# First mixture of experts of a two-layer decoder: order of the mask rows, wide maskings, and hidden values masked by TensorE

## The reference, cut to what matters

```
scores = sigmoid(x @ gate_w.T);  sel = top_2(scores + expert_bias)        # 8 experts
routed = x[token of each choice] * normalised_score
xq   = mxfp8_qdq(routed)                 # blocks of 32: power-of-two scale, float8 payload
h13  = ragged_dot(xq, w13q^T, counts);   h = silu(h1) * h3
hq   = mxfp8_qdq(h)
routed_out = ragged_dot(hq, w2q^T, counts)      # each row by the expert that it chose
shared = (silu(x @ sw1.T) * (x @ sw3.T)) @ sw2.T
out = shared + sum over the two choices of routed_out
```

## Time and profile before

| what | value |
|---|---|
| median of 3 runs | 1411.94 us (1411.03 to 1414.29) |
| profiled execution | 1419.62 us |
| its span | 1417.8 us |
| mean granted TensorE clock | 0.929 |
| busy share PE / DVE / ACT / POOL | 85% / 62% / 39% / 34% |

### The profile page before, as it was taken

How to read it: one execution, slowest core, us unless ns; L and a number is a source line. 1 busy time by engine, 2 the same in 40 slices (tenths; PEclk the granted TensorE clock), 3 DMA queues, 4 the chain that set the end, 5 groups by cost and what they waited for, 6 DMA issues and landing times.

```text
span 1417.8 us, 21841 instructions
## 1 busy us (share of the span) xinstructions
PE 1202.7 (85%) x7071; PEld 806.6 (57%) x7071; DVE 878.5 (62%) x2229; ACT 557.5 (39%) x1460; POOL 478.3 (34%) x584
## 2 busy tenths in 40 slices
PE   7688998999879959899999989998999409889881
PEld 3554664667744447466774356634667307777770
DVE  1677887753498993766637877587764523444443
ACT  2246776885351101377300167513772302212210
POOL 2253763743100002355400044301442362444444
PEclk9899999999969979899979999999999758999996
DMA  7065996000001001100030000003103523444544
GB/s 293 27 225 171 310 327 191 17 1 1 31 1 44 1 1 75 60 1 2 1 127 1 0 1 1 1 1 131 78 1 119 213 95 69 81 80 81 86 69 108
DMA packets 69612, 110.72 MB, mean 78 GB/s; under 512 B 5056, under 2 KB 59840, under 8 KB 66240
## 3 DMA queue, kind: packets, MB, share of 16 engines
q1 hardware_dynamic: 58896, 96.62, 20.2%
q0 software_dynamic: 10608, 12.72, 5.8%
HBM read 57.41 MB, written 51.91 MB: 77 GB/s over the span
## 4 chain that ended last, share of the span: by engine, by line
PE 66%; DVE 17%; issue 6%; POOL 4%; DMA 3%; ACT 2%; another core or an unknown queue 1%; SPq 1%; POOLq 0%; DVEq 0%; ACTq 0%
PE ps L701 8%; PE ps L690 6%; PE ps L979 6%; PE ps L710 4%; PE ps L682 4%; PE ps L683 3%; PE ps L1033 3%; PE ps L1030 3%; PE ps L960 2%; PE ps L650 2%; PE ps L812 2%; POOL mem L1839 2%; PE ps L864 2%; PE ps L884 2%; PE ps L1049 1%
## 5 line engine op out<-in xcount | busy, mean ns | idle before, releaser
L1839 POOL TENSOR_SCALAR mem<-mem 128x512 f32<-128x512 f32 x256 | 178.4, 701 | 383.9 <-DVE mem L1172 380.6
L1167 DVE TENSOR_REDUCE mem<-ps 128x1 f32<-128x512 f32 x256 | 175.2, 687 | 106.6 <-PE ps L683 98.1
L1665 ACT ACTIVATE mem<-ps,mem 128x512 f32<-128x512 f32 x256 | 177.3, 697 | 13.2 <-DVE mem L1167 12.6
L690 PE MATMUL ps<-mem 128*128 128x128 f32 x1024 | 158.0, 277 | 14.3 <-POOL mem L1839 13.4
L690 PEld LDWEIGHTS ps<-mem 128*128 128x128 f32 x1024 | 117.4, 140 | 69.2 <-POOL mem L1839 51.0
L1658 ACT ACTIVATE mem<-ps 128x512 f32<-128x512 f32 x192 | 116.2, 606 | 90.2 <-PE ps L690 89.7
L1890 POOL DMA_INDIRECT sums<-mem x63 | 97.1, 1542 | 133.1 <-DVE mem L1527 113.5
L682 PE MATMUL ps<-rounded_at 128*128 128x512 f32 x256 | 124.5, 486 | 10.9 <-DVE rounded_at L1156 10.4
L701 PE MATMUL ps<-mem 128*64 128x256 f32 x1024 | 124.6, 385 | 2.4 <-ACT mem L1658 2.4
L1633 ACT ACTIVATE rounded_at<-ps 64x512 fp32r<-64x512 f32 x64 | 37.9, 592 | 165.8 <-PE ps L962 153.0
L683 PE MATMUL ps<-rounded_at 128*128 128x512 f32 x256 | 102.3, 400 | 0.0
(11 more groups left out here) (259 smaller groups left out, 2464.0 us busy)
## 6 DMA issues: line engine op xcount, KB each, us to landing
slots<-mem SPq DMA_DIRECT2D x15, 2312.0 KB, 10.3
mem<-in_f_w_dram SPq DMA_DIRECT2D x16, 1024.0 KB, 9.0
mem<-slots SPq DMA_DIRECT2D x63, 136.0 KB
mem<-in_f_w_dram SPq DMA_DIRECT2D x24, 256.0 KB, 3.3
mem<-in_x_wq_dram SPq DMA_DIRECT2D x2, 2048.0 KB, 13.2
mem<-in_x_wo_dram SPq DMA_DIRECT2D x2, 2048.0 KB, 8.4
mem<-sums SPq DMA_DIRECT2D x8, 256.0 KB, 4.2
mem<-in_x_wqr_dram SPq DMA_DIRECT2D x1, 1536.0 KB, 6.7
```

The costliest lines, as they stand in the source:

```text
L690: mm = pe.transpose(ps[3 + j % 2][:, k * P:(k + 1) * P], PR[j % 6][:, k * P:(k + 1) * P], ident)
L1167: dve.tensor_reduce(nmax[:, i % 8:i % 8 + 1], ps[SB[lay][i % len(SB[lay])]][:, :], AX.X, ALU.max, negate=True)\
L1665: act.activation(PR[i % 6], ps[SB[lay][i % len(SB[lay])]][:, :], ACT.Exp, bias=nmax[:, i % 8:i % 8 + 1], accum_out=esum[:, i % 8:i % 8 + 1 ...
L1839: pool.tensor_scalar(PR[i % 6], PR[i % 6], rinv[:, i % 8:i % 8 + 1], 1.0, ALU.mult, ALU.mult)\
```

## The change

The change does these things, all in `experts_layer0` and what it calls:

- Mask rows are made in the order of the stretches (8 for s = 0, 8 for s = 1, 8 for s = 2, the last 8 in pairs between the first-layer tiles), instead of all 32 of choice 0 and then choice 1 ahead of everything.
- `masked(s)` is 2 DVE instructions of 128x4096 instead of 16 of 128x512. Both operands are repeated by broadcasting: the turned tokens over four experts, the mask rows over two halves of the width. Each half is signalled by itself, and `masked(0)` stands behind piece 2 instead of behind piece 4.
- The shared expert's four products are spread: two ahead, one behind tile 3, one behind tile 11. The other DVE steps are laid between them anew.
- `hidden_masked` on DVE, with `hidden_transposes` and the copy `turned`, is gone. In its place POOL turns mask rows that were used into diagonals: for each stretch and tile one product of 128x8x128 of the identity and the one-hot columns, written over `mrow` (16 in all). PE multiplies each quantised tile by these diagonals (`hidden_turned`: two matmuls of 512 columns for each half of the width, 64 in all), which turns and masks at once, and ACT copies the results, 128x1024 each, to `HM` (32 in all). Half of `hidden_turned` stands inside the output tiles t = 1 to 4.
- `hid0` gives the hidden products of each quantisation a buffer of their own.

```diff
+        def hidden_pair(q):
+            return pp[3 if q % 2 else 2 if q < 16 else 0]
...
+                for f in range(E0):
+                    mask_rows(f)
+                shared(0)
+                shared(1)
+                for f in range(E0, 2 * E0):
+                    mask_rows(f)
+                token_transposes(0)
+                for f in range(2 * E0, 3 * E0):
+                    mask_rows(f)
+                pe.wait_ge(f_sh, 2)
+                for w in range(16):
...
+                    if w in (1, 6, 9):
+                        token_transposes(w // 4 + 1)
+                    if w in (3, 11):
+                        shared(2 + w // 8)
+                    if 5 <= w < 9:
+                        mask_rows(3 * E0 + 2 * (w - 5))
+                        mask_rows(3 * E0 + 2 * (w - 5) + 1)
+                    if w in (13, 14):
+                        hidden_turned(0, 2 * (w - 13))
+                hidden_turned(1, 0)
+                hidden_turned(1, 2)
...
+            def hidden_turned(s, t0):
+                pe.wait_ge(q_d, NW8 + 8 + 2 * s + t0 // 2 + 1)
+                pe.wait_ge(f_diag, 4 * s + t0 + 2)
...
+                        if q >= 2:
+                            pe.wait_ge(f_hm, q - 1)
+                        for e in range(0, E0, 4):
+                            mm = pe.matmul(hidden_pair(q)[:, e * P:(e + 4) * P].rearrange("p (e s) -> p e s", e=4),
+                                           q8[:, s, t, c * P:(c + 1) * P],
+                                           mrow[:, j * E0 + e:j * E0 + e + 4, h * 512 + t * P:h * 512 + (t + 1) * P],
...
             def experts_layer0_out(t, bank):
-                pe.wait_ge(f_hm, 2 * (t // 4) + 2)
+                if 1 <= t <= 4:
+                    hidden_turned(2 + (t - 1) // 2, 2 * ((t - 1) % 2))
+                pe.wait_ge(f_hm, 16 * (t // 4) + 8 + 2 * (t % 4) + 2)
...
-                    for e in range(E0):
-                        for c in range(DC):
-                            last = dve.tensor_tensor(QM[s % 2][:, e, c, :], qT8[:, s, c, :],
-                                                     mrow[:, j * E0 + e, h * 512:(h + 1) * 512], ALU.mult)
-                    last.then_inc(f_qm, 1)
-                def hidden_masked(s):
...
+                    for e in range(0, E0, 4):
+                        dve.tensor_tensor(QM[s % 2][:, e:e + 4, :, :], qT8[:, s, :, :].unsqueeze(1).to_broadcast(wide),
+                                          mrow[:, j * E0 + e:j * E0 + e + 4, h * 512:(h + 1) * 512].unsqueeze(2).to_broadcast(wide),
+                                          ALU.mult).then_inc(f_qm, 1)
...
+                for s in range(4):
+                    j, h = s % 2, s // 2
+                    pool.wait_ge(f_qm, 2 * s + 2)
+                    for t in range(4):
+                        wide = [P, E0, P]
+                        pool.tensor_tensor(mrow[:, j * E0:(j + 1) * E0, h * 512 + t * P:h * 512 + (t + 1) * P],
+                                           identb.unsqueeze(1).to_broadcast(wide),
+                                           hot0b[:, j, 4 * h + t, :].unsqueeze(2).to_broadcast(wide), ALU.mult).then_inc(f_diag, 1)
```

## The result

| what | before | after |
|---|---|---|
| median of 4 timed runs each, run in turn | 1413.12 us (1411.03 to 1419.84) | 1430.08 us (1423.78 to 1431.75) |
| profiled execution | 1419.62 us | 1429.61 us |
| its span | 1417.8 us | 1427.8 us |

The ratio is 1.0087, with a 95% interval of 1.0054 to 1.0120: the changed kernel is slower, by 7.6 to 17.0 us. The quotient of the two medians, 1.0120, lies at the upper end of that. The forecast was 1428.6 us with a range of 1408 to 1437.

A forecast was written before the change was run, and what follows sets the result against it. It took DVE's list plus six output tiles on PE to bound the sublayer. A net +17.7 us from turns, less 1.0 from the rest, gave +16.7 on 1411.94: 1428.6 us, range 1408 to 1437.

The forecast's parts named there:

- turns: In the quantisations DVE and POOL alternate by whole instructions; products cost DVE 28.2 us, net 17.7 after waits; chance 58%.
- DVE's list: DVE's work in the sublayer gets 25.3 us shorter: four hidden maskings go, four token maskings take 4.4 us each.
- rival B: Wide masking products on DVE run at the slow rate, 8.8 us a masking: +6.6 us without turns, +34 with; 7%.
- POOL's product: Each of POOL's 16 diagonal products of 1024 elements takes 2.05 us.
- rival C: POOL's bf16 product is short, about 1.04 us, so the kernel is +2.7 us (1414.6); chance 8%.
- DVE's waits: DVE's waiting in the sublayer grows from 3.1 to 18.3 us, of which the turns take up 10.5.
- Turnings in the last tiles: On PE, three turnings at output tiles 2 to 4 follow the first addition, 3.0 us each, 9.1 in all.
- The signs it named: Trace readings if right: output tiles 2 to 4 7.6 us apart, wide masking 2.2, POOL products 2 to 2.8 us.
- the 518 at which the forecast would have fallen: DVE's last quantisation was to end near 533 us; ending before 518 us would make the forecast fall wholly.
- the line it pointed to: The quantisation's DVE product, L1222 before, was to have a mean well over 692 ns, single ones near 2.7 us.
- At no cost: New buffers and finer signals add no work; SP's loads for the next sublayer move later but are used from 556 us.
- A: POOL's products do not hold DVE up in the quantisations; kernel at 1406 to 1411 us, put at 1408.5; chance 27%.

The follow-up runs named there:

- the second measurement: The changed kernel timed and profiled once more with no edit: 1433.88 us, ratio 1.0092 to the kernel before.
- The two runs: The kernel before with all eight maskings as wide products (1410.08 us), and that plus two additions and the last hidden turning moved (1403.69 us).

## Why the prediction was right

The forecast (turns, +16.7 us) held in its mechanism. Its size came near in part by luck: it charged the turns 7.5 us too much, and let them take up 6.5 us too much of DVE's waits. By its steps:

- *DVE's list, -25.3 us.* Measured: 42.9 - 17.9 = 25.0. A pair of wide maskings takes 4.49 us where 4.4 was expected; rival B's slow rate (8.8) did not come.
- *POOL's product, 2.05 us.* Measured 1.97 on the mean of 16, and 1.89 to 1.94 where nothing holds it; rival C (1.04) did not come.
- *Turns, +28.2 us.* Measured: the excess of the five lines over their short means, times 16, is 5.7 (L1327: 701 less 346 ns) + 6.0 (L1246: 796 less 422) + 2.6 (L1248) + 4.8 (L1250) + 1.6 (L1252: 790 less 692) = 20.7 us. This term was mis-sized. The forecast charged a held instruction the whole of POOL's product. In fact L1246 at 416.35 had 0.23 us of the product behind it when it started, and of its own 0.43 us only 0.29 came after POOL's end: it cost 1.57, not 2.05. That some 0.14 us of a DVE instruction runs under POOL's could have been read in the earlier trace rows: L1205 takes 216 ns and ended only 0.07 to 0.08 us behind POOL. The four stretches cost 5.7, 4.0, 5.7 and 5.3 us where 7.5, 6.4, 7.5 and 6.8 were forecast. The second is the lowest because the first of its products ran in DVE's wait, which lasted until 438.77, and the second began beside the shared product L1298, which was not held: with one operand in PSUM it took its usual 0.69 us.

```profile
438.43 1.90 POOL L1911 TENSOR_TENSOR mem<-mem 128x1024 bf16<-128x1024 bf16 x1
...
438.77 0.69 DVE L1298 TENSOR_TENSOR mem<-ps,mem 128x512 f32<-128x512 f32 x1 [1.94 <-ACT mem L1718]
```

- *DVE's waits, 7.8 us with turns, 3.1 before.* Measured 12.0: 4.46 ahead of `masked(0)` (forecast 4.4) and 0.91 for a shared product ahead of it, 1.94 for the third shared product (forecast: gone), 1.52 ahead of `masked(3)` (0.9), and 3.21 for the last first-layer tile (2.5). The turns took up less of the waits than forecast. The run without diagonals has 16.0 us of waits (forecast without turns: 18.3), so the products took up 4.0 us, not 10.5. What POOL costs in the end is then 20.7 - 4.0 = 16.7 us (16.6 by the table: 180.2 - 163.6), where the forecast had 28.2 - 10.5 = 17.7: two errors that nearly cancel. The first addition comes 3.9 us later than before (528.80 against 524.89), where the forecast had 7.6. The terms give -25.0 + 20.7 + 8.9 = +4.6; the remaining 0.7 is taken to be fewer gaps.
- *Turnings in the last tiles, +9.1 us.* Measured 11.2: from the first work behind the addition to the last output row but two, 38.4 us (529.27 to 567.68) against 27.2 (525.50 to 552.71). Two turnings are 3.07 as forecast; the first is 3.9, and the tile behind it 1.2 us slower (1.91 and 3.95 against 1.03 and 3.66), at the granted clock of 0.50 shown above. The forecast had put "a little" for that in its range. Together with the 3.9 above this makes the sublayer's 15 us.
- *The signs it named.* Output tiles 2 to 4 are 7.6 us apart (538.88 to 546.53), the others 4.58; the wide masking shows 2.28; POOL's products show 1.89 to 2.34 (forecast 2 to 2.8). DVE's last quantisation ends at 528.88, not near 533, and after the 518 at which the forecast would have fallen. Wrong was the line it pointed to: L1222's own counterpart, L1255, stays at 692 ns, since four products in turn are over by L1250 or L1252, three or four instructions ahead of it. L1250 is the line that shows the turns (994 ns on the mean, against 691). Single ones reach 2.3 us, not 2.7.
- *At no cost:* SP's loads for the window attention moved into the stretch from 480 to 495 us, and from there to 571.31, where they are first used, there is time enough. The cover held.

```profile
480.00:495.00 15.00, 14.01 (x57) 5.83 (x57) 14.55 (x20) 5.52 (x8) 5.75 (x3) 1.00 0.31 103
```

The last two columns are the DMA share and 103 GB/s, where the earlier trace rows had next to nothing from 442.30 on.

The sublayer's end is 15.0 us later (571.04 against 556.06) where the sum had 16.7. That the median, 1430.08, lies only 1.5 above the forecast is luck: the ratio, from runs in turn, says +12.3 us, the second measurement +13.1, which is some 4 less than the forecast. The two profiles place these 4 us differently. In the first the sublayer is 14.8 us longer and the kernel gives back 4.8 behind it, which the forecast did not look for; in the second the sublayer itself is only 12.3 us longer and nothing is given back. Which of the two is usual stays open.

Of the rivals, A is refuted by the pair of runs without and with twice the products; B and C by one group each. The rule of the Trainium skill on which the forecast leaned (SBUF — State Buffer, Who interferes with whom: an exclusive lock on the shared pair of ports) agrees with the trace: a two-input DVE product of 0.69 us took 2.30 beside a POOL product of 1.89, and the reduction with one input kept its 0.69. The forecast charged every product nearly whole (28.2 / 16 = 1.8 us); the runs show 1.3 us a product (20.7 / 16). The two overlap at both ends, the reduction lets a part of one through, and the part of a product that meets a DVE wait, or a DVE product with an operand in PSUM, costs nothing.

## What to carry to other kernels

Work given to GpSimd is not free because GpSimd is idle: where VectorE bounds the stretch, price each GpSimd instruction that works in the shared memory as VectorE time, some two thirds of its own length here, and put it in a VectorE wait or on ScalarE instead. Before an operation is taken off the bounding engine altogether, try it as fewer, wider instructions; and look at what stands behind the last wait of a stretch, since moving two short additions and one turn ahead of long work (10.4 us in the sublayer, with the wide products) was worth more than removing 25 us from the engine's list (some 2 us once POOL was out of the way). The two runs differ by 5.8 us for the additions and the turn (10.4 - 4.6); moving them without the wide products was not run.

## What the runs showed of the hardware beyond that

- A DVE bf16 product with both operands repeated by broadcasting takes 2285 ns for 4096 elements, 0.56 ns each, so the repetition costs nothing that shows against plain operands (416 ns for 512, with the next starting after 335, 0.65 each).
- DVE's TENSOR_SCALAR, with one input in memory, is held by POOL like the products are (L1246: 2.00 us for 0.43). The reduction is not (0.69 under POOL's product at 418.02), nor is a product with one operand in PSUM (L1298: 0.69 beside the product at 438.43).
- POOL's product in bf16 (1.89 us for 1024 where nothing holds it) is not much shorter than in f32 (2.35 us for 1024, 1.04 for 512), and far from half.
- ACT takes 391 ns for a scaled bf16 copy of 128x128, and 1027 ns for a 128x1024 f32 copy from PSUM with scattered bf16 output, about the 1021 ns of the earlier trace rows for a bf16 source.
